# A decoder layer in one launch: shorter scale chains, the up factor's product moved, maxima and passes begun in pieces

## The reference, cut to what matters

```python
x = x + self_attention(layernorm(x))                       # causal, one head of 128
x = x + cross_attention(layernorm(x), context, mask)       # 16 heads of 8
x = x + ffn(layernorm(x))

def act_qdq(t):                                            # over the whole tensor
    qmax = 32767
    scale = maximum(max(abs(t)) / qmax, 1e-12)
    return clip(round(t / scale), -qmax - 1, qmax) * scale

def ffn(x):
    x    = act_qdq(x)
    up   = act_qdq(x @ lpbq(w_up).T)
    gate = act_qdq(x @ lpbq(w_gate).T)
    sig  = clip(round(sigmoid(gate) * 65536), 0, 65535) / 65536
    gate = act_qdq(gate * sig)
    o    = act_qdq(gate * up)
    return o @ lpbq(w_down).T
```

## Time and profile before

| | us |
|---|---|
| median of 3 runs (343.75 to 343.91) | 343.8 |
| the profiled execution | 344.55 |
| its span, first to last instruction | 342.8 |

### The profile page before, as it was taken

How to read it: one execution, slowest core, us unless ns; L and a number is a source line. 1 busy time by engine, 2 the same in 40 slices (tenths; PEclk the granted TensorE clock), 3 DMA queues, 4 the chain that set the end, 5 groups by cost and what they waited for, 6 DMA issues and landing times.

```text
span 342.8 us, 9760 instructions
## 1 busy us (share of the span) xinstructions
PE 304.8 (89%) x3697; PEld 203.7 (59%) x3697; DVE 276.4 (81%) x584; ACT 258.4 (75%) x461; POOL 184.3 (54%) x330
## 2 busy tenths in 40 slices
...
PEclk9999999999999999999999999999998999899999
...
GB/s 149 256 273 33 93 154 207 169 165 77 74 144 187 189 186 4 2 5 5 3 4 2 5 5 2 0 0 2 0 0 0 1 1 0 1 2 0 31 94 122
DMA packets 23752, 22.68 MB, mean 66 GB/s; under 512 B 3545, under 2 KB 21402, under 8 KB 23578
## 3 DMA queue, kind: packets, MB, share of 16 engines
...
q10 hardware_dynamic: 1536, 0.28, 0.4%
...
## 4 chain that ended last, share of the span: by engine, by line
PE 42%; DVE 28%; POOL 10%; ACT 8%; issue 7%; SPq 2%; ACTq 1%; DMA 1%; POOLq 0%; DVEq 0%
DVE mxs L1706 10%; DVE nm L1485 10%; PE banks L918 6%; PE banks L966 6%; PE banks L660 5%; PE banks L702 5%; PE banks L590 4%; PE banks L724 3%; PE banks L720 3%; PE banks L669 3%; POOL X L400 2%; PE banks L583 2%; POOL rstd L367 2%; DVE G L1764 1%; SPq L318 1%
## 5 line engine op out<-in xcount | busy, mean ns | idle before, releaser
L1485 DVE TENSOR_REDUCE nm<-banks 128x8 f32<-128x1024 f32 x64 | 78.3, 1223 | 11.0 <-PE banks L660 7.3
L1157 ACT ACTIVATE PT<-banks,bmask,vmask 128x1024 f32<-128x1024 f32 x64 | 77.0, 1202 | 1.8
L918 PE MATMUL banks<-X3T,upT 128*128 128x512 f32 x96 | 47.2, 639 | 12.5 <-DVE mxs L1706 7.7
L530 POOL TENSOR_TENSOR G<-ng,sq 128x1536 int32<-128x1536 int32 (+3 forms) x10 | 27.9, 2792 | 37.9 <-DVE sq L1731 37.9
L1706 DVE TENSOR_REDUCE mxs<-G 128x1 f32<-128x1536 int32 (+5 forms) x29 | 41.9, 1468 | 5.2 <-ACT G L1212 5.2
L918 PEld LDWEIGHTS banks<-X3T,upT 128*128 128x128 f32 x96 | 18.5, 202 | 39.4 <-issue 19.0
L702 PE MATMUL banks<-PT,VP 128*32 128x128 f32 x1024 | 41.2, 279 | 0.6 <-ACT wo L1147 0.3
L1001 ACT ACTIVATE h<-X,shift,rstd 128x128 f32<-128x128 f32 x64 | 26.3, 484 | 10.7 <-POOL shift L412 10.7
L660 PE MATMUL banks<-kd,qd 32*128 32x128 f16 x512 | 25.4, 216 | 5.7 <-DVE nm L1485 2.0
L702 PEld LDWEIGHTS banks<-PT,VP 128*32 128x32 f32 x1024 | 24.1, 109 | 9.3 <-issue 3.9
L454 POOL CAST NM<-nm 128x64 bf16<-128x64 f32 x32 | 7.6, 236 | 39.5 <-DVE nm L1485 39.5
...
## 6 DMA issues: line engine op xcount, KB each, us to landing
...
X3T<-m_dram SPq DMA_DIRECT2D x1, 1792.0 KB, 10.0
...
```

What stands on the lines that cost most here:

```text
L530: nc.gpsimd.tensor_tensor(GI[:, c], ng[:, u, part], sq[:, u, part], ALU.mult).then_inc(S["b_t"], 1)
L918: m = pe.matmul(bank(2 + FC * (g % 2) + k), w[:, k * P:k * P + P], grp(X3T, g), start=True, stop=True)
L1157: act.activation(PT[:, a, :], bank(2 + 2 * a, 2), ACT.Exp, bias=bmask[:, n:n + 1], scale=vmask[:, n:n + 1]).then_inc(S["t_exp"], 1)
L1485: V.tensor_reduce(nm[:, n % 2, 2 * NSET * a:2 * NSET * (a + 1)], bank(0, 2).rearrange("p (h m) -> p h m", m=P), AX.X, ALU.max, negate=True ...
```

## The change

- **Scale chains.** The last piece's maxima no longer pass through a reduce of all columns: the earlier columns are reduced ahead of it (`earlier_largest`) to mxe, already divided by 32767 and compared with a guard, and one operation (`steps_of_rows`) makes mxw from the last column and mxe. The guard 1e-12 is divided by `unit` beforehand (`guard_of`), so that step = max(mxa) needs no further operation: lev = 1 / step, and scale = step * unit beside it.
- **Up factor.** For tensor 2 ScalarE makes mxw, and scale[2] = step * unit (`scale_of(2)`) is computed behind the chain of tensor 3.
- **Pass 1.** Group 0 is rounded and multiplied in two halves of 256 columns. The maxima of group 6 are taken in three pieces, as those of group 7 were.
- **Last stage.** Group 0's first quarter is rounded by VectorE alone, group 1 goes in quarters and group 2 in halves. Group 2's products wait for the first result. The last maximum of pass 3 is one operation.
- **Attention's end.** The turned group 0 goes behind `queries(B - 1)`; `project(B - 3)` goes behind the scores of block 31; ScalarE's order of `max_copy(B - 1)` and `project_copy(B - 4)` is reversed, and `out_copy(B - 1)` and `turn_copy(B - 1)` each go one place up.
- Some semaphores of the setup are merged.

The diff, without the setup's semaphores and the allocations:

```diff
@@ -864,20 +864,20 @@
...
     both(n, 0)
-    if n == B - 1:
-        turn_early_rows3(0)
     pe.wait_ge(S["t_exp"], 2 * n + 2)
     pv(n, 1)
-    if n > 0:
+    if 0 < n and n != B - 2:
         project(n - 1)
     both(n, 1)
+    if n == B - 2:
+        project(n - 1)
...
 queries(B - 1)
-turn_early_rows3(1)
-turn_early_rows3(2)
+for g in range(3):
+    turn_early_rows3(g)
 turn(B - 1)
@@ -897,15 +897,13 @@
...
-def over_partitions(n, count, where):
-    pe.wait_ge(S["g_mx"], 2 * n)
-    for k in range(count):
-        m = pe.transpose(bank(where)[:, k * P:(k + 1) * P], mxw[:, k, :], ident[:, :])
-    m.then_inc(S["g_all"], 1)
+def over_partitions(n, where):
+    pe.wait_ge(S["g_mx"], n)
+    pe.transpose(bank(where)[:, 0:P], mxw[:, :], ident[:, :]).then_inc(S["g_all"], 1)
 pe.wait_ge(S["u_tc"], 1)
-over_partitions(1, 1, 2)
+over_partitions(1, 2)
 pe.wait_ge(S["t_xd"], 3)
@@ -918,10 +916,21 @@
...
+def half_hidden(h_, w):
+    part = slice(h_ * GT // 2, (h_ + 1) * GT // 2)
+    for k in range(FC):
+        m = pe.matmul(bank(2 + k)[:, part], w[:, k * P:k * P + P], X3T[:, part], start=True, stop=True)
+        if h_:
+            m.then_inc(S["a_g"], 1)
...
 pe.wait_ge(S["f_tc"], 1)
-for g in range(NG):
-    pe.wait_ge(S["a_n3"], g + 1)
+for h_ in range(2):
+    pe.wait_ge(S["a_n3"], 1 + h_)
+    half_hidden(h_, gateT)
+for g in range(1, NG):
+    pe.wait_ge(S["a_n3"], g + 2)
     for k in range(FC):
@@ -937,7 +946,7 @@
...
     if g == 0:
-        over_partitions(2, 1, 0)
+        over_partitions(2, 0)
     hidden(g, upT, (2,)).then_inc(S["b_u"], 1)
@@ -948,15 +957,15 @@
...
     if g == 0:
-        over_partitions(3, 1, 0)
+        over_partitions(3, 0)
     if g == 2:
-        over_partitions(4, 1, 1)
+        over_partitions(4, 1)
...
     idle_products(1, k)
-over_partitions(5, 1, 0)
+over_partitions(5, 0)
 idle_products(1, 9)
@@ -968,17 +977,23 @@
...
 pe.wait_ge(S["f_tc"], 3)
+for g in range(2):
+    for b in range(GB):
+        pe.wait_ge(S["d_on"], 1 + GB * g + b)
+        m = down(2 + g, g, b)
+    m.then_inc(S["d_y"], 1)
+pe.wait_ge(S["d_yc"], 1)
 for b in range(GB):
-    pe.wait_ge(S["d_on"], 1 + b)
-    m = down(2, 0, b)
+    pe.wait_ge(S["d_on"], 1 + 2 * GB + b // 2)
+    m = down(2, 2, b)
 m.then_inc(S["d_y"], 1)
-for g in range(1, NG - 1):
-    pe.wait_ge(S["d_on"], g + GB)
-    wait(pe, "d_yc", g - 1)
+for g in range(3, NG - 1):
+    pe.wait_ge(S["d_on"], g + 2 * GB)
+    pe.wait_ge(S["d_yc"], g - 1)
     for b in range(GB):
...
     m.then_inc(S["d_y"], 1)
-pe.wait_ge(S["d_on"], NG + GB - 1)
+pe.wait_ge(S["d_on"], NG - 1 + 2 * GB)
 for b in range(GB):
@@ -1167,11 +1182,9 @@
...
         out_copy(n - 1)
-    if n == B - 2:
-        max_copy(B - 1)
     if 1 < n < B - 1:
         project_copy(n - 2)
-    if n + 1 < B - 1:
+    if n + 1 < B:
         max_copy(n + 1)
@@ -1183,10 +1196,10 @@
...
+out_copy(B - 1)
 rows3_copy(0, 0)
-out_copy(B - 1)
+turn_copy(B - 1)
 rows3_copy(1, 1)
-turn_copy(B - 1)
 weights_copy(0, gateT, 0)
@@ -1198,7 +1211,8 @@
...
-    wait(act, "a_n3", g - 1)
+    if g > 3:
+        act.wait_ge(S["a_n3"], g)
     wait(act, "u_tca", g if g > 2 else 0)
@@ -1226,7 +1240,7 @@
...
-act.wait_ge(S["g_lev"], 2)
+act.wait_ge(S["g_sc"], 2)
 gate_levels(0, slice(0, GT))
@@ -1246,6 +1260,9 @@
...
+act.wait_ge(S["g_early"], 5)
+act.wait_ge(S["g_all"], 2)
+act.activation(mxw[:, :], bc(mx1[:, 2:3], [P, P]), ACT.Copy, scale=1.0 / AQ).then_inc(S["g_mx"], 1)
 act.wait_ge(S["g_lev"], 3)
@@ -1263,13 +1280,20 @@
...
 act.wait_ge(S["g_lev"], 5)
+def output_levels(g, part):
+    act.activation(oq[:, g % 2].rearrange("p (c t) -> p c t", c=FC)[:, :, part],
+                   GI[:, g * FW:(g + 1) * FW].rearrange("p (c t) -> p c t", c=FC)[:, :, part], ACT.Copy,
+                   scale=lev[:, 4:5]).then_inc(S["d_oq"], 1)
+for b in range(1, GB):
+    output_levels(0, slice(b * P, (b + 1) * P))
 for b in range(GB):
-    part = slice(b * P, (b + 1) * P)
-    act.activation(oq[:, 0].rearrange("p (c t) -> p c t", c=FC)[:, :, part],
-                   GI[:, 0:FW].rearrange("p (c t) -> p c t", c=FC)[:, :, part], ACT.Copy, scale=lev[:, 4:5]
-                   ).then_inc(S["d_oq"], 1)
-for g in range(1, NG):
-    wait(act, "d_on", g + 2 if g > 1 else 0)
+    output_levels(1, slice(b * P, (b + 1) * P))
+act.wait_ge(S["d_on"], GB)
+for h_ in range(2):
+    output_levels(2, slice(2 * h_ * P, 2 * (h_ + 1) * P))
+for g in range(3, NG):
+    act.wait_ge(S["d_on"], g + 2 * GB - 2 if g > 3 else 2 * GB)
     act.activation(oq[:, g % 2], GI[:, g * FW:(g + 1) * FW], ACT.Copy, scale=lev[:, 4:5]).then_inc(S["d_oq"], 1)
@@ -1598,6 +1622,17 @@
...
+def largest_of(k, cols):
+    V.tensor_reduce(mx1[:, k:k + 1], mxs[:, k, 0:cols], AX.X, ALU.max).then_inc(S["g_early"], 1)
+def earlier_largest(k, cols):
+    largest_of(k, cols)
+    dve.wait_ge(S["g_early"], 2 * k + 1 - (k > 2))
+    wait(dve, "g_guard", 2 * k)
+    V.tensor_scalar(mxe[:, k:k + 1], mx1[:, k:k + 1], 1.0 / AQ, guard[:, k:k + 1], ALU.mult, ALU.max
+                    ).then_inc(S["g_early"], 1)
@@ -1643,60 +1678,62 @@
...
 largest3(NG - 1, 2 * NG - 2, (2, 3))
+dve.wait_ge(S["u_mx"], 2 * NG - 1)
+earlier_largest(0, 2 * NG - 1)
 row3_last(3)
...
+def steps_of_rows(k, col):
+    dve.wait_ge(S["g_early"], 2 * k + 2 - (k > 2))
+    V.tensor_scalar(mxw[:, :], bc(mxs[:, k, col:col + 1], [P, P]), 1.0 / AQ, mxe[:, k:k + 1], ALU.mult, ALU.max
+                    ).then_inc(S["g_mx"], 1)
+def levels_from(k, where):
+    dve.wait_ge(S["g_all"], k + 1)
+    V.tensor_reduce(step[:, k:k + 1], bank(where)[:, 0:P], AX.X, ALU.max).then_inc(S["g_s"], 1)
+    dve.wait_ge(S["g_s"], k + 1)
+    V.reciprocal(lev[:, k:k + 1], step[:, k:k + 1]).then_inc(S["g_lev"], 1)
+    if k == 0:
+        V.tensor_copy(scale[:, 0:1], step[:, 0:1]).then_inc(S["g_sc"], 1)
+    elif k != 2:
+        scale_of(k)
+def scale_of(k):
+    dve.wait_ge(S["g_unit"], k)
+    V.tensor_tensor(scale[:, k:k + 1], step[:, k:k + 1], unit[:, k:k + 1], ALU.mult).then_inc(S["g_sc"], 1)
+def guard_of(k):
+    dve.wait_ge(S["g_unit"], k)
+    V.reciprocal(runit[:, k:k + 1], unit[:, k:k + 1]).then_inc(S["g_guard"], 1)
+    dve.wait_ge(S["g_guard"], 2 * k - 1)
+    made, factor = (mxs[:, k, 2 * NG - 1:2 * NG], 1e-12 * AQ) if k in (2, 4) else (guard[:, k:k + 1], 1e-12)
+    V.tensor_scalar(made, runit[:, k:k + 1], factor, None, ALU.mult).then_inc(S["g_guard"], 1)
...
-n_scale, n_unit = [0], [0]
-def next_units(*made):
...
-    scales_from(k0, k1, where)
-scales(0, 1, 2)
+steps_of_rows(0, 2 * NG - 1)
+levels_from(0, 2)
 dve.wait_ge(S["g_lev"], 1)
...
-for g in range(2):
-    dve.wait_ge(S["u_tca"], g + 1)
-    V.tensor_scalar(n3m[:, g], grp(X3T, g), lev[:, 0:1], MAGIC, ALU.mult, ALU.add).then_inc(S["a_rnd"], 1)
-    dve.wait_ge(S["a_rnd"], g + 1)
-    V.tensor_scalar(grp(X3T, g), n3m[:, g], -MAGIC, None, ALU.add).then_inc(S["a_n3"], 1)
-next_units(V.tensor_copy(unit[:, 1:2], scale[:, 0:1]), V.tensor_copy(unit[:, 2:3], scale[:, 0:1]),
-           V.tensor_scalar(unitq[:, 1:2], scale[:, 0:1], 1.0 / AQ, None, ALU.mult),
-           V.tensor_scalar(unitq[:, 2:3], scale[:, 0:1], 1.0 / AQ, None, ALU.mult))
+def first_levels(n, g, part):
+    rows = X3T[:, g * GT + part.start:g * GT + part.stop]
+    V.tensor_scalar(n3m[:, g, part], rows, lev[:, 0:1], MAGIC, ALU.mult, ALU.add).then_inc(S["a_rnd"], 1)
+    dve.wait_ge(S["a_rnd"], n)
+    V.tensor_scalar(rows, n3m[:, g, part], -MAGIC, None, ALU.add).then_inc(S["a_n3"], 1)
+dve.wait_ge(S["u_tca"], 1)
+first_levels(1, 0, slice(0, GT // 2))
+first_levels(2, 0, slice(GT // 2, GT))
+dve.wait_ge(S["u_tca"], 2)
+first_levels(3, 1, slice(0, GT))
+dve.wait_ge(S["g_sc"], 1)
+for k in (1, 2):
+    V.tensor_copy(unit[:, k:k + 1], scale[:, 0:1]).then_inc(S["g_unit"], 1)
@@ -1707,17 +1744,23 @@
...
 levels(3)
-for g in range(NG - 1):
+guard_of(1)
+guard_of(2)
+for g in range(NG - 2):
     dve.wait_ge(S["a_gc"], FC * g + FC)
...
         levels(g + 4)
-for k in range(FC):
-    g = NG - 1
+for k in range(2 * FC):
+    g = NG - 2
     dve.wait_ge(S["a_gc"], FC * g + k + 1)
+    if k == 2 * FC - 1:
+        dve.wait_ge(S["a_mx"], g + k)
+        earlier_largest(1, g + k)
     largest(1, g + k, G[:, g * FW + k * GT:g * FW + (k + 1) * GT], "a_mx")
-dve.wait_ge(S["a_mx"], NG + 2)
-scales(1, 2, 0)
+dve.wait_ge(S["a_mx"], NG - 2 + 2 * FC)
+steps_of_rows(1, NG - 3 + 2 * FC)
+levels_from(1, 0)
@@ -1734,9 +1777,9 @@
...
-dve.wait_ge(S["g_lev"], 2)
-next_units(V.tensor_scalar(unit[:, 3:4], scale[:, 1:2], 1.0 / 65536.0, None, ALU.mult),
-           V.tensor_scalar(unitq[:, 3:4], scale[:, 1:2], 1.0 / 65536.0, 1.0 / AQ, ALU.mult, ALU.mult))
+dve.wait_ge(S["g_sc"], 2)
+V.tensor_scalar(unit[:, 3:4], scale[:, 1:2], 1.0 / 65536.0, None, ALU.mult).then_inc(S["g_unit"], 1)
+guard_of(3)
 sigmoid_levels(0, slice(0, GT), 1)
@@ -1744,20 +1787,26 @@
...
     if g == NG - 1:
-        scales_from(2, 3, 0)
+        levels_from(2, 0)
     silu_largest(g - 1)
...
         dve.wait_ge(S["b_umx"], NG)
-        row_maxima(2, 3)
```

(64 more changed lines are left out.)

38 lines of the change are left out of this document (6 added, 32 removed).

## The result

The changed kernel took 341.85 us in the median of 12 executions (340.46 to 343.70), the kernel before beside it 344.07. The ratio is 0.994, 95% interval 0.9921 to 0.9960: 2.1 us faster, where 3.2 were forecast. Timed again with later runs it gave 342.73 (340.63 to 343.83) and 0.9949 (0.9926 to 0.9973), 1.8 us faster.

A forecast was written before the change was run, and what follows sets the result against it. Chained waits bound the kernel: TensorE in pass 1 and the last stage, VectorE's maxima in passes 2 and 3, small operations at four seams. Shifts of -0.25, -0.64, -1.49 and -0.86 sum to -3.24: median 340.6 us, range 339.7 to 342.3.

The forecast's parts named there:

- the case that I gave 0.66: Whole kernel: the forecast itself, all terms together -3.24 us, median 340.6 us; chance 0.66.
- rival A: Up factor's seam: TensorE's clock falls where TensorE is the bound, one stretch costs half of 3.4 us: 342.3; chance 0.10.
- a low clock at either place: Sign of being wrong: TensorE at its low clock in the groups at the up factor's seam or in the last stage.
- Attention's end: Seam from attention to pass 1: block 31's turn comes later behind four more transposes, +0.22 us.
- First scale: Before pass 1: a shorter chain from the last maximum to the first rounding, -0.30 us.
- Halves: Start of pass 1: rounding 256 columns instead of 512 brings the first product earlier, -0.17 us.
- Seam 2: Between passes 1 and 2: earlier widening and a shorter chain behind TensorE, -0.64 us.
- Seam 3: Between passes 2 and 3: the up factor's lev no longer stands for GpSimd's product, silu step earlier, -1.49 us.
- Last stage: From the last scale to the end: earlier first product and fewer waits of TensorE, -0.86 us.

The follow-up runs named there:

- experiment 1: The changed kernel with 7 idle products in TensorE's stream ahead of the transpose of the up factor's maxima: 340.26 us, ratio 0.9883 to the kernel before.
- experiment 7: The kernel before with the edits at attention's end alone: 344.42 us, ratio 0.9997 to the kernel before.

## Why the prediction was right, and what was off

The time lay in the range, and the way from the seams to the sum held. But the case that I gave 0.66 did not come about. What came was rival A, which I had given 0.10 and priced at 342.3, and "a low clock at either place" was among my own signs of being wrong. The other terms together brought 0.67 more than forecast, and this made up for part of the 1.67 that the clock took. That the median is only some 1.2 off 340.6 is in this part luck.

The bounds were also added up wrongly. The best of all terms sum to -4.48, so 339.3 and not 339.6, the worst to -1.50, so 342.3 and not 342.0; with A on top of the worst it would be 344.0. In the last stage 339.97 stands for the 339.95 of the earlier trace rows, 0.02 too much. 341.85 lies inside either way. Step by step:

- **Attention's end** (+0.22, measured -0.06). The mis-sized term is what stood before block 31's turn. I had taken it as ready exactly when the eight transposes ended, and a further four as 0.52. The early start was right (pv 0.28 earlier against the root), but the twelve took 1.47, so the four 0.43, and in the kernel before the turn had started only when the eight were over: in the changed kernel it comes 1.31 behind the first transpose (215.86 and 214.55), before 1.05 (216.37, and 215.32 of the earlier trace rows). 0.26 later against 0.28 earlier.
- **First scale** (-0.30, measured -0.47). The early pair fitted in full, and the reciprocal follows the reduce sooner than the scale operation did. VectorE's timeline, to be set beside the earlier trace rows:

```profile
218.45 0.17 DVE L1627 TENSOR_REDUCE mx<-mxs 128x1 f32<-128x15 f32 x1
218.66 0.21 DVE L1634 TENSOR_SCALAR mxe<-mx,guard 128x1 f32<-128x1 f32 x1
...
218.83 0.35 DVE L1615 TENSOR_SCALAR X<-X,mvar,rstd 128x128 f32<-128x128 f32 x1
...
219.53 0.29 DVE L1690 TENSOR_SCALAR mxw<-mxs,mxe 128x128 f32<-128x128 f32 x1
...
220.30 0.29 DVE L1696 TENSOR_REDUCE step<-banks 128x1 f32<-128x128 f32 x1 [0.48 <-PE banks L903]
...
220.62 0.16 DVE L1698 RECIPROCAL lev<-step 128x1 f32<-128x1 f32 x1
220.70 0.14 DVE L1700 COPY scale<-step 128x1 f32<-128x1 f32 x1
...
220.82 0.35 DVE L1725 TENSOR_SCALAR n3m<-X3T,lev 128x256 f32<-128x256 f32 x1
```

  The widening takes 0.29, 0.06 over the copy; the scale's copy costs 0.01 and not 0.07.
- **Halves** (-0.17, measured -0.26): 256 columns took 0.35 and 0.29, at the better bound; the second lies below the 0.35 that I had taken as the least. The idle products in front were hardly a floor: the first product starts 0.16 behind the rounding's end, before 0.14.
- **Seam 2** (-0.64, measured -0.55): right in sum, not in its parts. Ahead of the reduce behind TensorE I forecast -0.27 and -0.09 came (1.86 from the table load before, 1.77 after), since VectorE still ends 1.04 behind ScalarE's last copy. Behind that reduce I forecast -0.37 and -0.46 came (1.04 to the gate's step before, 0.58 after).
- **Seam 3** (-1.49, measured +0.04 with the clock down, -1.63 with the wait filled). The mechanism and its size were right: -1.64 at the up step in the changed kernel, -1.77 and +0.14 at up and silu step in experiment 1. What failed is the assumption that TensorE would stay at full clock, and with it the chance of rival A: I gave 0.10 to what both profiles show. My reason against it was the full speed at this place in one profile of the kernel before, behind a wait only 0.07 shorter; in experiment 7 the same code has the fall there behind 1.96. And I named only the fall behind 3.30 of idle. The first of the two 8s of the earlier trace rows is another one, behind a wait as short as the seam's, and TensorE's timeline of the kernel before has it:

```profile
258.49 7.31 PE L918 MATMUL banks<-X3T,upT 128*128 128x512 f32 x12 [2.08 <-DVE mxs L1706]
```

  Its price, half of 3.4 us, was right (1.67). The Trainium skill, "TensorE: Matmul & The Clock Gate", section "HAM oscillation — how this bites in real kernels", named with the rival, has every burst behind a long wait for data begin at the low clock. The trace agrees in part only: the burst behind the 2.04 did, those behind pass 2's waits of 1.49 to 2.08 in the same profile did not.
- **Last stage** (-0.86, measured -0.97): the idle products set the start and the pieces took the waits, 0.58 by experiment. Group 2 waits for nothing.

By the marks' distances the whole is -2.24 in the profile; 0.50 more is the earlier arrival at attention's end. With the seam's clock kept it would be -3.91. The four kernels with seven idle products and nothing else changed but idle products were timed at 0.9883 to 0.9902, 3.4 to 4.0 us under the kernel before; -3.24 (0.9906) was forecast.
